# The node states of later graph pairs reach hT through VectorE turns and a DRAM scratch instead of TensorE transposes

## The reference

```
h = x
for i in range(4):
    hw = einsum('bnc,cd->bnd', h, weight[i])
    m  = einsum('bjn,bjd->bnd', adj, hw)          # adj is 1024 x 1024 of zeros and ones
    gx = m @ w_ih[i].T + b_ih[i];  gh = h @ w_hh[i].T + b_hh[i]
    r = sigmoid(xr + hr);  z = sigmoid(xz + hz);  n = tanh(xn + r * hn)
    h = (1 - z) * n + z * h
out = layernorm(x + h * mask)                     # over the 128 features
```

## Time and profile before

| | |
|---|---|
| median of three runs | 546.95 us (546.69 to 547.09) |
| the profiled execution | 549.29 us, of it 547.5 us of span |
| TensorE busy | 515.9 us (94%) |
| VectorE, ScalarE, GpSimd busy | 397.9, 375.4, 218.8 us |
| TensorE's granted clock, mean | 0.988 of full speed |
| moved by DMA | 80.93 MB |

### The profile page before, as it was taken

How to read it: one execution, slowest core, us unless ns; L and a number is a source line. 1 busy time by engine, 2 the same in 40 slices (tenths; PEclk the granted TensorE clock), 3 DMA queues, 4 the chain that set the end, 5 groups by cost and what they waited for, 6 DMA issues and landing times.

```text
span 547.5 us, 7461 instructions
## 1 busy us (share of the span) xinstructions
PE 515.9 (94%) x2288; PEld 420.4 (77%) x2288; DVE 397.9 (73%) x695; ACT 375.4 (69%) x616; POOL 218.8 (40%) x161
## 2 busy tenths in 40 slices
PE   5898999999999999999999999999999999999950
PEld 4566888888888888788888888888888788888740
DVE  3997767666689786666699886666779886666666
ACT  2855777747786787875886877874886677664422
POOL 0034344443245554333345644233354545244332
PEclk9999999999999999999999999999999999999995
DMA  7952256164662165373662156365472122323302
GB/s 225 389 215 77 88 210 222 53 179 136 199 222 78 62 227 196 109 215 117 196 248 75 59 209 214 111 187 158 134 270 81 55 77 78 116 93 123 108 25 80
DMA packets 79808, 80.93 MB, mean 148 GB/s; under 512 B 3656, under 2 KB 63648, under 8 KB 79776
## 3 DMA queue, kind: packets, MB, share of 16 engines
q1 hardware_dynamic: 79504, 80.41, 44.6%
q10 hardware_dynamic: 272, 0.13, 0.1%
HBM read 60.08 MB, written 20.45 MB: 147 GB/s over the span
## 4 chain that ended last, share of the span: by engine, by line
PE 78%; DVE 9%; DMA 5%; issue 3%; ACT 3%; SPq 2%; POOL 1%; DVEq 0%; ACTq 0%; POOLq 0%
PE p_S L472 34%; PE p_r L482 5%; PE p_r L486 5%; PE p_r L483 5%; PE p_z L482 5%; PE p_z L486 5%; PE p_z L483 5%; PE p_hn L482 2%; PE p_hn L483 2%; PE p_hn L486 2%; PE p_xn L486 2%; PE p_xn L482 2%; PE p_xn L483 2%; DMA bounce<-work 2%; DMA adj_in<-in_adj_dram 2%
## 5 line engine op out<-in xcount | busy, mean ns | idle before, releaser
L1256 POOL TENSOR_TENSOR work<-hT,work 128x512 f32<-128x512 f32 x63 | 87.5, 1390 | 259.8 <-ACT work L676 259.8
L472 PE MATMUL p_S<-adj_hi,nat_hi 128*128 128x512 f32 x480 | 187.4, 391 | 0.0
L472 PE MATMUL p_S<-adj_hi,nat_lo 128*128 128x512 f32 x480 | 186.8, 389 | 0.0
L472 PEld LDWEIGHTS p_S<-adj_hi,nat_hi 128*128 128x128 f32 x480 | 90.1, 188 | 18.9 <-DVE nat_lo L848 0.3
L472 PEld LDWEIGHTS p_S<-adj_hi,nat_lo 128*128 128x128 f32 x480 | 90.1, 188 | 18.5
L1137 DVE SCALAR_TENSOR_TENSOR work<-p_hn,bias,work 128x512 f32<-128x512 f32 x62 | 46.5, 749 | 79.4 <-ACT work L676 79.2
L1260 POOL TENSOR_TENSOR work<-work 128x512 f32<-128x512 f32 x63 | 90.4, 1434 | 4.9
L676 ACT ACTIVATE work<-p_r,bsum 128x512 f32<-128x512 f32 x63 | 43.3, 687 | 63.2 <-PE p_r L486 61.9
L676 ACT ACTIVATE work<-work,bias 128x512 f32<-128x512 f32 x63 | 45.7, 726 | 41.5 <-DVE work L1141 36.2
L905 DVE STREAM_TRANSPOSE work<-hT 128x512 f32<-128x512 f32 x62 | 69.1, 1114 | 2.1
L621 ACT ACTIVATE adj_hi<-adj_in 128x1024 fp32r<-128x1024 f32 x60 | 60.3, 1050 | 0.5 <-DMA adj_in<-in_adj_dram 0.4
(11 more groups left out here) (148 smaller groups left out, 925.6 us busy)
## 6 DMA issues: line engine op xcount, KB each, us to landing
adj_in<-in_adj_dram SPq DMA_DIRECT2D x64, 512.0 KB, 6.3
bounce<-work SPq DMA_DIRECT2D x62, 256.0 KB, 2.0
low<-bounce SPq DMA_DIRECT2D x62, 256.0 KB, 2.8
x_in<-in_x_dram SPq DMA_DIRECT2D x8, 512.0 KB, 6.7
y<-in_x_dram SPq DMA_DIRECT2D x8, 512.0 KB, 4.3
out_dram<-y SPq DMA_DIRECT2D x7, 512.0 KB, 4.1
y<-in_L_gnn_w_ih_dram SPq DMA_DIRECT2D x2, 192.0 KB, 3.4
y<-in_L_gnn_w_hh_dram SPq DMA_DIRECT2D x2, 192.0 KB, 4.3
```

Of the source, the lines that this page charges most:

```text
L472: last = nc.tensor.matmul(p_S[h][:, :], part[:, s, j], adj_hi[:, s, j, half(h)], start=(j == 0 and part is nat_hi), stop=(j == NB - 1 and ...
L1256: nc.gpsimd.tensor_tensor(t_sb[:, h], hT[:, s, half(h)], n_sb[:, h], ALU.subtract).then_inc(d_sub, 1)
```

## The change

For the first pair nothing changes in how `hT` is made. For the later pairs `transpose_x` is gone, and `x` goes another way:

- SP loads `x` once more into `x_in`, with eight consecutive nodes in each partition (`load_rows`, steps 1 and 2 of the pair before).
- VectorE turns it in 32x32 blocks from `x_in` into `y` (`turn_x`, two instructions per graph, in steps 5 and 6).
- SP writes `y` to the scratch `x_bounce` (`send_x`, steps 6 and 7) and reads it from there into `hT` with four transfers of 32 partitions each (`bring_xT`: graph 0 at the end of step 7, graph 1 in step 0 of the next pair).
- `take_xT` on ScalarE waits for that read and splits `hT` itself. GpSimd no longer adds high and low for these pairs.
- The natural load of `x_in` comes after `send_x`, in steps 6 and 7, not in step 5. The load of `y` for the residual comes later too: graph 0's in step 6 after two adjacency blocks, graph 1's in step 0 of the next pair behind `bring_xT`. In the last pair both stay where they were.

```
@@ SP
+            def load_rows(p, s, first):
+                if first:
+                    sp.wait_ge(x_tr, 2 * s + 2)
+                sp.wait_ge(xnat_lo, 2 * p + s + 1)
+                sp.dma_start(x_in[:, s], xrows_v[2 * p + 2 + s]).then_inc(xrows_loaded[s], 16)
+            def send_x(p, s):
+                sp.wait_ge(x_turned, 4 * p + 2 * s + 2)
+                sp.dma_start(x_bounce[s], y[:, s].rearrange("p a b -> p (a b)")).then_inc(x_out[s], 16)
+            def bring_xT(s, pairs_out):
+                sp.wait_ge(x_out[s], 16 * pairs_out)
+                for q in range(Q):
+                    sp.dma_start(hT[q * 32:(q + 1) * 32, s].rearrange("r (m f) -> r m f", m=Q),
+                                 x_bounce[s].rearrange("(m r) (q f) -> q r m f", m=Q, q=Q)[q]).then_inc(x_back[s], 16)
+            def load_x(p, s):
+                sp.dma_start(x_in[:, s], x_v[2 * p + 2 + s]).then_inc(x_loaded[s], 16)
...
+                    if g == 0 and not first:
+                        bring_xT(1, p)
+                        sp.dma_start(y[:, 1], x_v[2 * p - 1]).then_inc(y_loaded[1], 16)
+                    if g in (1, 2) and not last:
+                        load_rows(p, g - 1, first)
...
                     elif g == STEPS - 2:
-                        load_y(p, 1, first)
-                    if last:
-                        pass
-                    elif g == 5:
-                        for s in range(2):
-                            sp.wait_ge(x_tr, 4 * p + 2 * s + 2)
-                            sp.wait_ge(xnat_lo, 2 * p + s + 1)
-                            sp.dma_start(x_in[:, s], x_v[2 * p + 2 + s]).then_inc(x_loaded[s], 16)
-                    elif g == STEPS - 2:
-                        next_adj(p, 1, first, range(0, 2))
-                    elif g == STEPS - 1:
+                        if last:
+                            load_y(p, 1, first)
+                        else:
+                            send_x(p, 0)
+                            load_x(p, 0)
+                            next_adj(p, 1, first, range(0, 2))
+                            sp.wait_ge(x_out[0], 16 * (p + 1))
+                            load_y(p, 0, first)
+                    elif g == STEPS - 1 and not last:
+                        send_x(p, 1)
+                        load_x(p, 1)
                         next_adj(p, 1, first, range(2, NB))
+                        bring_xT(0, p + 1)
@@ TensorE
-                    if g < 2 and not (first and g == 0):
+                    if first and g == 1:
                         transpose_x(p, g, first)
@@ ScalarE, take_xT (VectorE's reads hT instead of p_tr likewise)
+                if not first:
+                    act.wait_ge(x_back[s], 16 * Q * p)
+                    act.wait_ge(hn_done, HS * (p - 1) + 2 * (STEPS - 2 + s) + 2)
                 for h in range(2):
-                    act.wait_ge(x_tr, 4 * p + 2 * s + h + 1)
-                    copy(hT_hi[:, s, half(h)], flat(p_tr[h])).then_inc(xT_hi, 1)
+                    if first:
+                        act.wait_ge(x_tr, 2 * s + h + 1)
+                    copy(hT_hi[:, s, half(h)], flat(p_tr[h]) if first else hT[:, s, half(h)]).then_inc(xT_hi, 1)
@@ VectorE
+            def turn_x(p, s, n, first):
+                dve.wait_ge(xrows_loaded[s], 16 * (p + 1))
+                if not first:
+                    dve.wait_ge(out_stored[s], 16 * p)
+                rows = slice(n * HB, (n + 1) * HB)
+                nc.vector.transpose(y[:, s].rearrange("p a b -> p (a b)").rearrange("p (q a j) -> p j q a", q=Q, j=NB)[:, rows],
+                                    x_in[:, s, rows].rearrange("p j (q c) -> p j q c", q=Q)).then_inc(x_turned, 1)
...
+                            if g in (STEPS - 3, STEPS - 2) and not last:
+                                turn_x(p, g - (STEPS - 3), 0, first)
...
+                    if g in (STEPS - 3, STEPS - 2) and not last:
+                        turn_x(p, g - (STEPS - 3), 1, first)
@@ GpSimd
-                    if l == 0:
+                    if l == 0 and first:
```

More of the change, by code:

```diff
@@ L105, in gnn_kernel @@
         bounce = nc.dram_tensor("bounce", [2, P, H], F32, kind="Internal").ap()
+        x_bounce = nc.dram_tensor("x_bounce", [2, P, N], F32, kind="Internal").ap()
         turned = work[:, 0]
@@ L149, in gnn_kernel @@
         x_tr = sem("x_tr")
+        xrows_loaded = [sem(f"xrows_loaded{s}") for s in range(2)]
+        x_turned = sem("x_turned")
+        x_out = [sem(f"x_out{s}") for s in range(2)]
+        x_back = [sem(f"x_back{s}") for s in range(2)]
         xT_hi = sem("xT_hi")
@@ L216, in gnn_kernel @@
         x_v = x.rearrange("b (j p) c -> b p j c", p=P)
+        xrows_v = x.rearrange("b (p j) c -> b p j c", p=P)
         out_v = out.rearrange("b (j p) c -> b p j c", p=P)
@@ L337, in body @@
                     elif g == 4:
-                        if first:
-                            sp.wait_ge(start_tr, L)
-                        else:
+                        if not first:
                             store(p - 1, 0)
@@ L345, in body @@
                             store(p - 1, 1)
-                        load_y(p, 0, first)
+                        if last:
+                            load_y(p, 0, first)
                     elif g == STEPS - 2:
-                        load_y(p, 1, first)
-                    if last:
-                        pass
-                    elif g == 5:
-                        for s in range(2):
-                            sp.wait_ge(x_tr, 4 * p + 2 * s + 2)
-                            sp.wait_ge(xnat_lo, 2 * p + s + 1)
-                            sp.dma_start(x_in[:, s], x_v[2 * p + 2 + s]).then_inc(x_loaded[s], 16)
-                    elif g == STEPS - 2:
-                        next_adj(p, 1, first, range(0, 2))
-                    elif g == STEPS - 1:
+                        if last:
+                            load_y(p, 1, first)
[4 more added lines that the diff above has]
+                            sp.wait_ge(x_out[0], 16 * (p + 1))
+                            load_y(p, 0, first)
+                    elif g == STEPS - 1 and not last:
+                        send_x(p, 1)
+                        load_x(p, 1)
                         next_adj(p, 1, first, range(2, NB))
+                        bring_xT(0, p + 1)
             pairs(sp, body)
@@ L657, in split_x, with take_xT @@
                 copy(nat_hi[:, s], x_in[:, s]).then_inc(xnat_hi, 1)
-            def take_xT(p, s):
+            def take_xT(p, s, first):
+                if not first:
+                    act.wait_ge(x_back[s], 16 * Q * p)
+                    act.wait_ge(hn_done, HS * (p - 1) + 2 * (STEPS - 2 + s) + 2)
                 for h in range(2):
-                    act.wait_ge(x_tr, 4 * p + 2 * s + h + 1)
-                    copy(hT_hi[:, s, half(h)], flat(p_tr[h])).then_inc(xT_hi, 1)
+                    if first:
+                        act.wait_ge(x_tr, 2 * s + h + 1)
+                    copy(hT_hi[:, s, half(h)], flat(p_tr[h]) if first else hT[:, s, half(h)]).then_inc(xT_hi, 1)
             def take_back(p, g, h):
@@ L762, in body @@
                     if l == 0 and not early:
-                        take_xT(p, s)
+                        take_xT(p, s, first)
                     s_high(p, g, 0)
@@ L813, in _ @@
                 if j == NB - 2:
-                    take_xT(0, 0)
+                    take_xT(0, 0, True)
                 take_adj(0, 0, j)
@@ L890, in check_adj, with take_xT @@
                                         ALU.bitwise_or).then_inc(adj_checked, 1)
-            def take_xT(p, s):
+            def take_xT(p, s, first):
                 for h in range(2):
                     dve.wait_ge(xT_hi, 4 * p + 2 * s + h + 1)
-                    lo(hT_lo[:, s, half(h)], flat(p_tr[h]), hT_hi[:, s, half(h)]).then_inc(xT_done, 1)
+                    lo(hT_lo[:, s, half(h)], flat(p_tr[h]) if first else hT[:, s, half(h)],
+                       hT_hi[:, s, half(h)]).then_inc(xT_done, 1)
+            def turn_x(p, s, n, first):
+                dve.wait_ge(xrows_loaded[s], 16 * (p + 1))
+                if not first:
+                    dve.wait_ge(out_stored[s], 16 * p)
+                rows = slice(n * HB, (n + 1) * HB)
+                nc.vector.transpose(y[:, s].rearrange("p a b -> p (a b)").rearrange("p (q a j) -> p j q a", q=Q, j=NB)[:, rows],
+                                    x_in[:, s, rows].rearrange("p j (q c) -> p j q c", q=Q)).then_inc(x_turned, 1)
             def take_adj1(j):
```

## The result

| | before | changed |
|---|---|---|
| median | 547.0 us | 590.4 us (589.6 to 591.7, 4 runs) |
| ratio to before | | 1.077 (95% interval 1.075 to 1.080) |
| profiled execution, and its span | 549.3, 547.5 us | 591.7, 590.1 us |
| TensorE busy | 515.9 us (94%) | 525.8 us (89%) |
| mean granted clock | 0.988 | 0.948 |

The kernel is slower by 43 us. The forecast was 580 us with a range to 596. The place and the two things waited for were as forecast, and the size was a quarter too small: 33 us more were forecast, 43 measured.

A forecast was written before the change was run, and what follows sets the result against it. TensorE, busy 94%, was taken to bound the kernel. New waits for `hT_hi` and `hT_lo`, net of the removed transposes and an old 1.3 us wait, add 11.2 + 10.4 + 11.7 = 33.3 us to 547.0: 580 us, range 562 to 596.

The forecast's parts named there:

- What bounds the kernel, and that every wait counts: TensorE, 47 to 520 us: waits only 1.6 us, so each cycle taken from it or new wait counts in the run.
- What is taken away, "4.1 us": Later pairs' transposes on TensorE: 0.87 us gained in step 0 and 0.5 in step 1, three times, 4.1 us.
- VectorE's turns, 0: Steps 5 and 6: two turns per graph fit in VectorE's free time and cost 0, upper end 6 us.
- SP's list and the first wait: Pair's end, steps 7 and 0: queued transfers delay the read into `hT` to 288.4; TensorE stands 7.7 us for `hT_hi`.
- Second wait: Steps 0 and 1: VectorE waits 3 to 5 us for `y`, so TensorE waits 3 to 4.4 us for `hT_lo`.
- The slow clock is hidden in it: Step 0's gates start at 1.2 GHz after the first wait, costed 1.5 us, but hidden in the second wait.
- The sum: L486 of step 1 comes 11.2, 10.4 and 11.7 us later in three pair starts: 33.3 us more, median 580.
- Hidden and faster: Pair's end: the read into `hT` lands below 281, 4.1 us are gained, 543 us; chance 0.06.
- Only the first wait: Pair start: `y` lands in time, 2.9 us less are lost per pair, 571 us; chance 0.12.
- The queue has room: SP's queue: half of the added bytes slip into gaps, 3.2 us less per pair, 570 us; chance 0.12.
- Narrow reads at half rate: Four 32-partition reads into `hT` run at half rate: 3.2 us per pair, 9.6 in all, 590 us; chance 0.12.
- Turns that come through: Steps 5 and 6: VectorE's turns are dear and come through, 586 us; chance 0.06.

The follow-up runs named there:

- The experiment with `y` alone: Kernel before, TensorE transposes kept, with only the two loads of `y` moved to where the changed kernel has them: 565.2 us, ratio 1.033.
- The fillers: Changed kernel with matmuls nobody reads put into TensorE's waits: 589.9 us with 36 in step 0, 587.9 us with 7 more in step 1.
- the run with 36: Changed kernel with 36 more matmuls nobody reads between aggregation and gates of step 0 of the later pairs: 589.9 us, ratio 1.077.
- the best order and a second queue: Changed kernel with SP's transfers reordered, what is needed first ahead, and `send_x` and `bring_xT` on GpSimd's queue: 559.3 us, ratio 1.022.
- VectorE's list was shortened: Kernel before without the later pairs' transposes, and VectorE's first four statistics of graph 0 moved from step 0 to step 1: 545.0 us, ratio 0.995.
- the run with both fillers: Changed kernel with 36 unread matmuls in step 0 and 7 more in step 1 ahead of the wait for `hT_lo`: 587.9 us, ratio 1.073.

## Why the prediction was right, and where it was off

**What bounds the kernel, and that every wait counts:** each new wait counted, but "a cycle taken from TensorE is a cycle of the run" was wrong at a pair's start. TensorE's 94% hid that VectorE's list, with the waits in it, is as long there.

**What is taken away, "4.1 us":** mis-sized. The transposes bring nothing measurable by themselves (548.2 against 547.95 us). It did not spoil the sum, which was made up to L486 of step 1 (L515 in the changed kernel) from the landing of `y` and not from this term.

**VectorE's turns, 0:** right, shown by doing them twice.

**SP's list and the first wait:** right in kind. In the second pair's end ScalarE had the read at 305.92, which is 290.1 after taking off the 15.8 us of shift; the forecast was 288.4. So TensorE stood 9.5 us and not 7.7. The load of `y` ahead of `bounce` made `bounce` take 5.9 us (278.73 to 284.62) in place of 4.2; that was forecast (1.6). `send_x` was issued 2.25 us later than the first block of before (288.68 less 15.8, against 270.63), of which 1.6 were priced. From there to 306.46, 17.8 us, the queue carried nine transfers of 512 KB and one of half that; at 1.58 us for 512 KB and 1.9 us till the first bytes (3.5 less 1.58) that is 16.9.

**Second wait:** right in its cause, a load of `y` that comes late. VectorE had `y` at 317.72, 301.9 by the other's clock, against a forecast of 299.9; 11.8 us behind the read where 11.5 were forecast. TensorE's L515 came at 327.51, 21.6 us behind the read against 21.1. TensorE's own wait there was mis-sized, 1.8 us against 3 to 4.4: it had stood 0.7 us for a block of `adj_hi` and begun slow, so it came to L515 later itself, and VectorE set the time either way. In the third pair nearly all of it was the 1.9 us for `adj_hi`, which the forecast did not have. The experiment with `y` alone shows this wait without the first.

**"The slow clock is hidden in it":** half wrong. The one behind the first wait is hidden by what the trace shows: VectorE stood 2.9, 3.2 and 4.5 us for `y` after it, more than the 1.9 us by which step 0's gates took longer (10.1 us from 306.68 on, where the kernel before took 8.2), and SP's list decides when `y` comes. The fillers do not show it by themselves, since the clock fell all the same in the run with 36. But TensorE's clock fell a second time, behind the second wait of 1.8 us, and nothing hides that in the first two pairs: step 1's gates took 1.7 us longer (step 2 starts at 337.08, 9.6 us behind L515, and at 306.83 in the kernel before, 7.9 behind its L486 at 298.96). This was not in the sum. In the third pair the clock fell behind the wait for `adj_hi`, inside the aggregation, and that was hidden: VectorE's `hT_lo` still came 0.2 us after TensorE was there.

**The sum.** The three pair starts lost 14.9, 14.4 and 12.2 us (step 2's aggregation starts at 197.16, 337.08 and 476.69 us, and at 181.03, 306.83 and 434.31 in the kernel before, less the shift that was there already) against 11.2, 10.4 and 11.7. What the second one lost beyond the forecast splits into 1.7 for the later read, 0.5 for the rest of the way to L515 and 1.7 for the clock. The first is like it, and the third, with 0.5 over the forecast, had no slow clock to pay for. 1.3 us more were lost in the start-up of this one execution, which the change does not explain.

**The rivals.** Hidden and faster: out. Only the first wait: out, VectorE stood for `y` in all three pairs, and the late `y` alone costs 18 us. The queue has room: out, the load of `y` ahead of `bounce` cost its 1.6 us, and the stretch of 17.8 us was longer than a full queue's 16.9. Narrow reads at half rate: out as a price of 9.6 us; 590 was met, but by other causes. What the Trainium skill (SBUF — State Buffer, Door 1: The DMA port swizzle) says of 32 partitions may hold for a transfer alone, which no run here shows. Here the queue was full of other transfers, and a plain read saved little more than what its issues cost. Turns that come through: out.

**Open:** the 11 us per run that remain with the best order and a second queue. TensorE's waits for `hT_hi` are 8.9 us; in all three pair starts ScalarE stands for an adjacency block (1.4 to 2.3 us) just before it comes to `hT_hi`. That the extra bytes make the blocks late is likely and not shown; no run left the bytes out there. A kernel that moves `x` in a quiet step, with a buffer of its own, was not tried.

## What to carry to other kernels

Before work is taken from the busiest engine, look at how long the next engine's list is over the same stretch: here VectorE's was as long with the waits in it, and 5.2 us of TensorE's work were worth nothing measurable till VectorE's list was shortened, and 2.5 us then. A transfer in an in-order list costs what stands behind it: price each move by the queue's fill at that moment, and follow the list one step further, since removing the first wait shows the next one behind the same bytes. A wait can show up under another name: the late `y` reached TensorE as a wait for `adj_hi`, through ScalarE's list. An early issue is no early landing.

## What the runs showed of the hardware

- TensorE's granted clock fell to the 1.2 GHz level behind a wait of only 1.8 us (at 327.51; before it TensorE had stood 0.7 us some 3 us earlier; the window 326 to 328 has PE busy 0.49 of 2 us, the window behind it clock 0.50). In the third pair it fell behind a single wait of 1.9 us after 15 us without one (row below). In the run with both fillers it stayed at 1.00 behind a wait of 2.2 us (at 165.98). So here the length of one wait did not decide it.
- Instructions of VectorE's residual (128x128, f32) took 0.34 to 0.35 us with GpSimd idle and up to 1.46 us where a product of GpSimd's overlapped them.
- Four reads of 32 partitions cost 1.7 us per pair more than one plain read each, 1.4 of it issues, with the queue full.
- With the reads on GpSimd's queue, a transfer of 256 KB on SP's queue took 4.6 us where a like one took 2.9.

```profile
463.82 0.50 PE L501 MATMUL p_S<-adj_hi,nat_hi 128*128 128x512 f32 x1 [1.91 <-ACT adj_hi L650]
```
